# Two edits to the axis stages of a convolution and scan kernel: the sigmoids' bias as an immediate, and eight more pairs folded into scaled triangles

## The reference, cut to what matters

```
dA = einsum('bld,dn->bldn', delta, A)
dB_u = einsum('bld,bld,bln->bldn', delta, u, B)
c = flip(cumsum(flip(shift(dA)), axis=1)); c = exp(min(c, 15))
x = cumsum(dB_u * c, axis=1) / (c + 1e-06)
y = einsum('bldn,bln->bld', x, C)
```

## Time and profile before

| what | value |
|---|---|
| runs | 17880.17, 17881.85, 17891.42 us; median 17881.85 |
| span of the profiled execution | 17874.5 us, 7.35 us under the median |
| granted clock of PE over the span | 0.984 of full speed |
| busy share of the span | DVE 95%, PE 88%, ACT 88%, POOL 88% |
| the `w_` stage's passes | 64, first and last DVE copy of dx at 8895.2 and 16217.7 us |
| one pass, 12272.62 to 12388.27 us | 115.65 us |

### The profile page before, as it was taken

How to read it: one execution, slowest core, us unless ns; L and a number is a source line. 1 busy time by engine, 2 the same in 40 slices (tenths; PEclk the granted TensorE clock), 3 DMA queues, 4 the chain that set the end, 5 groups by cost and what they waited for, 6 DMA issues and landing times. The chain is left out here.

```text
span 17874.5 us, 307595 instructions
## 1 busy us (share of the span) xinstructions
PE 15666.8 (88%) x66328; PEld 8928.0 (50%) x66424; DVE 16925.9 (95%) x45263; ACT 15656.0 (88%) x24641; POOL 15706.1 (88%) x10824
## 2 busy tenths in 40 slices
PE   8878898888888888888788888888888888888788
PEld 3325555555555555555455555555555555553233
DVE  7999999999999999999999999999999999997799
ACT  7769999999999999999799999999999999995588
POOL 4669999999999999999799999999999999996577
PEclk9999999999999999999899999999999999999899
DMA  2011011111011110111100000000000000000000
GB/s 41 16 19 11 9 11 12 12 11 11 9 12 12 11 12 10 10 12 11 13 11 12 12 9 12 12 12 12 11 10 11 12 12 11 12 11 12 21 16 14
DMA packets 785299, 227.32 MB, mean 13 GB/s; under 512 B 755377, under 2 KB 758093, under 8 KB 783437
## 3 DMA queue, kind: packets, MB, share of 16 engines
q1 hardware_dynamic: 780084, 204.64, 9.2%
q10 hardware_dynamic: 3352, 2.14, 0.1%
HBM read 143.66 MB, written 62.96 MB: 12 GB/s over the span
## 5 line engine op out<-in xcount | busy, mean ns | idle before, releaser
L1409 POOL TENSOR_TENSOR h_sm<-h_sm,h_wr 128x768 f32<-128x768 f32 x2944 | 5396.2, 1833 | 448.9 <-DVE h_wr L1134 348.7
L1409 POOL TENSOR_TENSOR w_sm<-w_sm,w_wr 128x768 f32<-128x768 f32 x2944 | 5395.3, 1833 | 369.3 <-DVE w_wr L1134 261.2
L1134 DVE SCALAR_TENSOR_TENSOR h_wr<-h_pz,h_bct,h_rbuf 128x192 f32<-128x192 f32 x11776 | 4292.3, 416 | 92.5 <-PE h_pz L1586 75.3
L1134 DVE SCALAR_TENSOR_TENSOR w_wr<-w_pz,w_bct,w_rbuf 128x192 f32<-128x192 f32 x11776 | 4292.2, 417 | 90.9 <-PE w_pz L1586 74.8
L1586 PE MATMUL h_pz<-h_xr,h_tri 128*128 128x384 f32 x6912 | 3079.1, 528 | 582.2 <-DVE h_wr L1134 469.9
L1586 PE MATMUL w_pz<-w_xr,w_tri 128*128 128x384 f32 x6912 | 3069.2, 526 | 571.8 <-DVE w_wr L1134 468.3
L1259 ACT ACTIVATE w_cbuf<-w_pe_e,w_consts 128x1024 f32<-128x1024 f32 x2304 | 2573.9, 1117 | 567.2 <-PE w_pe_e L1565 423.4
L1259 ACT ACTIVATE h_cbuf<-h_pe_e,h_consts 128x1024 f32<-128x1024 f32 x2304 | 2573.4, 1117 | 559.6 <-PE h_pe_e L1565 413.5
L1108 DVE SCALAR_TENSOR_TENSOR h_xr<-h_cbuf,h_bct,h_pdx 128x192 f32<-128x192 f32 x6912 | 2547.1, 413 | 150.5 <-ACT h_cbuf L1259 98.1
L1108 DVE SCALAR_TENSOR_TENSOR w_xr<-w_cbuf,w_bct,w_pdx 128x192 f32<-128x192 f32 x6912 | 2546.5, 413 | 133.4 <-ACT w_cbuf L1259 98.1
L1297 ACT ACTIVATE w_rbuf<-w_pe_e,w_consts 128x1024 f32<-128x1024 f32 x2304 | 2579.8, 1120 | 18.4 <-DVE w_wr L1134 16.0
(11 more groups left out here) (379 smaller groups left out, 27336.4 us busy)
## 6 DMA issues: line engine op xcount, KB each, us to landing
h_lt<-pieces_s SPq DMA_DIRECT2D x512, 96.0 KB, 4.9
w_lt<-pieces_s SPq DMA_DIRECT2D x512, 96.0 KB, 4.3
pieces_s<-h_pieces SPq DMA_DIRECT2D x384, 48.0 KB, 2.1
pieces_s<-w_pieces SPq DMA_DIRECT2D x384, 48.0 KB, 2.1
h_xt<-first_s SPq DMA_DIRECT2D x34, 128.0 KB, 6.3
w_xt<-first_s SPq DMA_DIRECT2D x34, 128.0 KB, 3.1
m_u<-hn_s SPq DMA_DIRECT2D x32, 128.8 KB, 2.7
m_u<-slots_s SPq DMA_DIRECT2D x32, 128.8 KB, 2.6
```

Of the source, the lines that this page charges most:

```text
L1134: ins = v.scalar_tensor_tensor(dst, pz[:, P % 2, m * DX:(m + 1) * DX], bct[:, par, g * 2 * NX + NX + n + m:g * 2 * NX + NX + n + m + 1], r ...
L1409: tt(sm[:, g], sm[:, g], wr[:, u % 3], ALU.add).then_inc(s_add, 1)
```

## The change

Two things change. The sigmoids get their bias as a number in the instruction, so `consts` shrinks from three columns to the one that the normalisation needs, with two memsets fewer at the start of a stage. And `WIDE` grows from 24 to 32 pairs of a pass: 3, 19, 35, 51, 67, 83 and 26, 74 are added; none of them is in `OTHER`. For these eight, DVE does one tensor_tensor instead of two scalar_tensor_tensor, ACT makes two scaled triangles each, PE does two matmuls of 192 columns instead of one of 384. The ring of triangles has four places instead of three, so `triangles` waits for the sums of the pair four back in the list. `triangles` (unchanged) makes a chunk's first triangle pair in part 0 and all others in part 1.

```
-        consts = sb("consts", [128, 3])
+        consts = sb("consts", [128, 1])
...
-        tb = sb("tb", [128, 3, 2, TB])
+        tb = sb("tb", [128, 4, 2, TB])
...
-        WIDE = [P for P in range(PAIRS) if P % 8 in (1, 5)]
+        WIDE = [P for P in range(PAIRS) if P % 8 in (1, 5) or P % 16 == 3 or P in (26, 74)]
         SCALED = WIDE
-        NS2, RING = len(SCALED), 3
+        NS2, RING = len(SCALED), 4
...
-                v.memset(consts[:, 0:1], C_BIAS)
-                v.memset(consts[:, 1:2], R_BIAS)
-                step(v.memset(consts[:, 2:3], 1e-5))
+                step(v.memset(consts[:], 1e-5))
...
-                                 ACT.Sigmoid, bias=consts[:, 0:1]).then_inc(s_c, 1)
+                                 ACT.Sigmoid, bias=C_BIAS).then_inc(s_c, 1)
...
-                                 ACT.Sigmoid, bias=consts[:, 1:2], scale=-1.0).then_inc(s_r, 1)
+                                 ACT.Sigmoid, bias=R_BIAS, scale=-1.0).then_inc(s_r, 1)
```

More of the change, by code:

```diff
@@ L1193, in _ @@
                 act.wait_ge(s_w, 16 * NW)
-                a.activation(bsc[:, 3:4], bn[:, 3:4], ACT.Ln, bias=consts[:, 2:3]).then_inc(s_ac, 1)
+                a.activation(bsc[:, 3:4], bn[:, 3:4], ACT.Ln, bias=consts[:]).then_inc(s_ac, 1)
                 act.wait_ge(s_ac, 1)
```

## The result

| | before | after |
|---|---|---|
| time, median (lowest to highest) | 17,881.01 us (17,879.85 to 17,891.42), 4 runs | 17,718.88 us (17,691.61 to 17,730.47), 4 runs |
| ratio after to before | | 0.9906, 95% interval 0.9892 to 0.9920 |
| span of the profiled execution | 17,874.5 us | 17,689.8 us |

The change makes the kernel 162 us faster by the medians, 185 us by the two profiled spans. The forecast was 17,680, the range 17,600 to 17,770. After's four runs lie 39 us apart, before's 12.

The account below looks back on a forecast made before the run. DVE, busy 112.31 of 115.65 us, was taken to pace the pass, with waits for PE and ACT in stretches. 0.38 + 0.65 + 0.57 = 1.60 us a pass, x 128 = 205 us, gave 17,680 us; range 17,600 to 17,770.

Parts of the forecast that it names:

- ACT's stretch: Chunk 5's c2 to chunk 8's: 19 shorter sigmoids less two triangle pairs bring pair 64 0.65 us earlier a pass.
- Pairs 3 and 19: First stretch of the pass, where DVE runs without gaps: two cheaper DVE products count in full, 0.38 us a pass.
- Pairs 26 and 35: Where DVE waits for PE's sums: DVE's saving becomes longer waits, counted 0, with 0.38 us as the other bound.
- where PE leads: Pairs 22 to 32 and 35 to 41: PE also has the next tile's projections and DVE waits for it.
- The column's price: Bias column on each of ACT's 72 sigmoids: costs 0.08 to 0.12 us, 0.095 taken.
- no relief on ACT: Rival: overlap hides the column's fetch, sigmoids get no faster; +0.21 us a pass, +27 us, 17,909; chance 0.08.
- Pairs 67, 74 and 83: Behind pair 64, late in the pass: three cheaper DVE products count in full, 0.57 us a pass.
- PE or POOL takes up the end of the pass: Rival: POOL's products limit the second half, so pairs 67, 74, 83 give nothing; 1.03 us a pass, 17,750; chance 0.15.
- a wait that the prediction named as a sign of being wrong: Chunks 8 and 9: PE waiting for POOL's products would show the forecast wrong.
- The slack of 0.57 us: Pair 79: POOL's product is ready 0.57 us before PE uses it; 0.19 left after 0.38 from pairs 67 and 74.

Follow-up runs that it names:

- all_31: Changed kernel with the bias matmul of the next tile's dt projection one turn earlier (turn 31, not 32): 17,612.58 us, ratio 0.9853.
- pairs_only: Changed kernel with the sigmoids' bias as a column again, keeping the eight pairs and the ring of four: 17,900.22 us, ratio 1.0015.
- all_31_column: Changed kernel with the dt projection's bias matmul one turn earlier and the sigmoids' bias as a column again: 17,824.78 us, ratio 0.9964.
- The four-pair versions: Changed kernel with only 3, 19, 74, 83 of the eight pairs: 17,705.24 us; with the bias matmul one turn earlier too: 17,665.46 us.
- bias_four: Changed kernel with only pairs 3, 19, 74 and 83 of the eight added: 17,705.24 us, ratio 0.9905.
- bias_only_31: Changed kernel cut back to the immediate bias alone (24 pairs, ring of three), with the bias matmul one turn earlier: 17,709.61 us, ratio 0.9907.

## Why the prediction was right, and where its terms were off

The lead of a pass can be followed along DVE. The table has the start of the first weighting of a pair after the copy of dx, the median over the plain passes of the second stage (49 before, 44 after).

| pair | before, us | after, us | lead | lead by the prediction |
|---|---|---|---|---|
| 18 | 22.74 | 22.36 | 0.38 | 0.38 (pairs 3, 19) |
| 24 | 29.83 | 29.27 | 0.56 | |
| 26 | 31.98 | 31.60 | 0.38 | 0.38 (26 given back) |
| 34 | 41.85 | 41.26 | 0.59 | |
| 38 | 46.38 | 45.98 | 0.40 | 0.38 (35 given back) |
| 62 | 76.80 | 75.82 | 0.98 | 1.03 (ACT's stretch) |
| 70 | 86.17 | 85.01 | 1.16 | 1.22 (67) |
| 72 | 88.58 | 87.24 | 1.34 | 1.41 (74) |
| 80 | 97.31 | 96.02 | 1.29 | 1.41 |
| 94 | 112.81 | 111.32 | 1.49 | 1.60 (83) |

*Pairs 3 and 19*: 0.38, as counted.

*Pairs 26 and 35*: each gives 0.19 to 0.21 and loses it at the next place where PE leads, 26 at the weighting of pair 25 (wait 0.11 to 0.30 us), 35 at that of pair 37 (0.07 to 0.26). The count of 0 was right, and so was its reason: with the bias matmul out of that stretch (all_31) the wait at 37 goes, pair 35 counts, and pair 26 is still swallowed.

*The column's price*: 0.093 us from the starts of the sigmoids, 0.095 taken. The Trainium skill, "ScalarE: Activation LUTs", section "What ACT_TABLE_LOAD costs", gives 93 ns for it, and the trace agrees; the reading by which an overlap of activations hides it does not hold here, and with it the rival *no relief on ACT*. That rival's sign is nonetheless what pairs_only shows: without relief on ACT the pairs are a loss, 0.43 us a pass measured, 0.21 worked out.

*ACT's stretch*: the lead grows by 0.58 us between pairs 38 and 62, predicted 0.65. With 0.093 for 0.095 the same sum gives 0.61; the last 0.03 stay unexplained. all_31_column and pairs_only are the direct tests: the column makes 1.72 us between pairs 38 and 62, and 19 x 0.093 are 1.77; the triangles make 1.16, and 2 x 0.58 are 1.16.

*Pairs 67, 74 and 83*: 0.51 us, 0.57 counted. 67 and 74 are in the table with 0.18 each; behind 74 the lead falls by 0.05, where PE now waits 0.17 and 0.23 us for POOL's products. This is the rival *PE or POOL takes up the end of the pass* in a small form, and a wait that the prediction named as a sign of being wrong. The slack of 0.57 us was less than what DVE came earlier, 1.34 us at pairs 72 to 76; by the prediction's own terms it would have been 0.38 + 0.65 + 0.38 = 1.41, and its sentence on the rival set only the last 0.38 against the slack. That the term held even so is in part luck: POOL, which the prediction took to get no faster, is released earlier by DVE in the first 57 us of the pass, and its product of pair 79 starts 92.61 us after the copy of dx and not 93.14. No sentence of the prediction counts these 0.53 us. The four-pair versions reach the rival in full.

*From the pass to the time*: 1.49 us a pass x 128 = 191 us by plain passes, 184 by the mean pass (116.40 to 114.96), 185 by the spans. The prediction's sum was 205, so 14 us are the terms above, and about 7 lie in the passes that are not plain, the half-clock ones among them. The medians differ by 162. The runs that were not profiled show mean granted clocks of 0.981 to 0.983 against 0.984 in the profiled one, and the lower clock goes with the longer time; that these are more half-clock passes is argued, not read from a trace of those runs. The spread as such has other sources too: bias_four, with 29 such passes, has runs 7 us apart, bias_only_31, with none, 24.

Still open: why some passes get the half-clock stretch and others not, with the same idle time and the same bias matmul ahead of it in all of them (see below). A stretch at half clock also follows the loop's back edge (its jump back to the start), which comes every sixth pass, in all kernels, though not each time; nothing was tried on it. That the scan and POOL's product hold one another up is read from the traces, and no run changes their order alone.

## What to carry to other kernels

A column operand is a cost that every instruction of the group pays, and it is worth the sum over the stretch in which that engine sets the time, not over the whole pass: 19 of 72 sigmoids decided here. Follow the lead of the critical engine along the pass, in a table of starts before and after; it shows which saving is swallowed where, and by whom. And when several engines are near 90% busy, expect parts of a change not to add: here one part alone gave 1.13 us, the other alone lost 0.43, and together they gave 1.49, until POOL became the next limit. A busy share of 89% did not show that limit; the place of POOL's last wait in the pass did.

## What the runs showed of the hardware

- An idle time of PE of 0.84 us with a short bias matmul behind it was followed, in 18 to 71 of 126 passes of six kernels, by 3.4 us at half the granted clock (1.2 GHz), which made the pass 1.6 to 1.7 us longer. Filling that idle time with the same bias matmul left none. Which of the idle time and the narrow matmul counts was not separated, and the two together are not enough: the idle time is 0.84 to 0.88 us with the same matmul behind it in passes with and without the stretch, and pairs_only has it in 6 passes alone, all right behind the loop's back edge.
- A scan on DVE and a product on POOL, both from SBUF, hold one another up: 0.94 and 1.83 us, or 1.49 and 1.00 with 2.48 for POOL's next addition, depending on 0.24 us in the order of their starts. The Trainium skill, "SBUF — State Buffer", section "Who interferes with whom", says that a VectorE instruction with two SBUF inputs contends with a GpSimd instruction that reads SBUF. The traces agree that one of the two is held up: a scan that starts 0.20 to 1.00 us after the product ends 1.81 to 1.83 us after the product's start in every pass of the fourteen kernels. Which one is held did not follow the order of starts in the profile, since a product that started up to 0.12 us ahead was the one to be stretched in 334 of 388 passes.
